# Q and K through the score banks, x2 rebuilt in the expert tiles, plain scatters, and idle products at the head

## The reference

```python
def _lora_proj(x, W, b, A, B):
    return einsum('bsh,oh->bso', x, W) + b + 2.0 * einsum('bsr,or->bso', einsum('bsh,rh->bsr', x, A), B)

q, k, v = proj(layernorm(x)), proj(ctx), proj(ctx)                     # 16 heads of 16
scores = einsum('bqhd,bkhd->bhqk', qh * D ** -0.5, kh) + attn_bias     # attn_bias: 128 x 16 x 128 x 128
attn = einsum('bhqk,bkhd->bqhd', softmax(scores, axis=-1), vh)
x2 = x + tanh(g_xattn[0]) * attn
xf = layernorm(x2)
idx = argmax(softmax(xf @ Wg + bg), axis=-1)                           # one of 8 experts
y = gelu(xf @ W1[idx] + b1[idx], approximate=False) @ W2[idx] + b2[idx]
out = x2 + tanh(g_ffn[0]) * y
```

## Time and profile before

| | us |
|---|---|
| median of 3 runs | 1670.7 (1669.65 to 1671.39) |
| the profiled execution | 1668.51 |
| its span, first to last instruction | 1666.6 |
| first product of scores | 57.73 after the span's start |
| first product of scores of sequence 124 | 1247.33 |
| last product with W1 | 1646.89 |
| PE busy | 1450.7, 87% of the span |
| DVE busy | 1061.8, 64% |
| ACT busy | 887.9, 53% |
| POOL busy | 942.9, 57% |

### The profile page before, as it was taken

How to read it: one execution, slowest core, us unless ns; L and a number is a source line. 1 busy time by engine, 2 the same in 40 slices (tenths; PEclk the granted TensorE clock), 3 DMA queues, 4 the chain that set the end, 5 groups by cost and what they waited for, 6 DMA issues and landing times.

```text
span 1666.6 us, 43159 instructions
## 1 busy us (share of the span) xinstructions
PE 1450.7 (87%) x13374; PEld 1166.7 (70%) x13374; DVE 1061.8 (64%) x2734; ACT 887.9 (53%) x1883; POOL 942.9 (57%) x671
## 2 busy tenths in 40 slices
PE   3789999989989989989998998998997589999886
PEld 2577777777777777777777777777776468777775
DVE  2477787787788788778778778778877311111111
ACT  1466666666666666666666666666664123333231
POOL 2345555555555555556555555555555356666667
PEclk9999999999999999999999999999999699999998
DMA  4355655555555555555555555555552499999994
GB/s 140 85 164 150 178 163 154 171 170 153 166 175 152 163 174 156 160 175 157 157 174 163 157 168 168 155 167 171 154 166 66 139 249 253 242 226 229 230 221 93
DMA packets 383026, 281.53 MB, mean 169 GB/s; under 512 B 21599, under 2 KB 349691, under 8 KB 382972
## 3 DMA queue, kind: packets, MB, share of 16 engines
q1 hardware_dynamic: 356092, 246.22, 50.8%
q0 software_dynamic: 26880, 34.64, 10.5%
HBM read 226.86 MB, written 56.00 MB: 170 GB/s over the span
## 4 chain that ended last, share of the span: by engine, by line
PE 51%; ACT 18%; DMA 15%; issue 10%; DVE 2%; SPq 1%; POOL 1%; ACTq 1%; POOLq 0%; DVEq 0%
DMA out<-og,ids 14%; PE bank L464 9%; PE bank L553 7%; PE bank L569 7%; PE bank L559 7%; ACT KT L642 5%; PE bank L515 5%; PE bank L451 4%; ACT OT L674 4%; ACT x2n L651 3%; ACT xn L651 3%; PE bank L519 3%; ACT PT L658 2%; PE bank L536 2%; PE bank L598 2%
## 5 line engine op out<-in xcount | busy, mean ns | idle before, releaser
L380 POOL TENSOR_TENSOR sc<-sc,negmax 128x1024 f32<-128x1024 f32 x256 | 484.4, 1892 | 435.6 <-DVE negmax L784 435.6
L778 DVE TENSOR_TENSOR sc<-bank,sc 128x512 f32<-128x512 f32 x512 | 337.6, 684 | 195.2 <-PE bank L451 192.4
L658 ACT ACTIVATE PT<-bank 128x512 f32<-128x512 f32 x512 | 293.3, 603 | 59.7 <-PE bank L464 59.7
L784 DVE TENSOR_REDUCE negmax<-sc 128x8 f32<-128x1024 f32 x256 | 312.3, 1220 | 17.0
L420 POOL DMA_INDIRECT out<-og,ids x144 | 223.5, 1552 | 132.3 <-issue 112.0
L464 PE MATMUL bank<-cst,sc 128*128 128x128 f32 x2048 | 273.6, 277 | 0.7 <-ACT PT L658 0.7
L464 PEld LDWEIGHTS bank<-cst,sc 128*128 128x128 f32 x2048 | 226.6, 142 | 43.1 <-issue 41.8
L943 DVE TENSOR_SCALAR og<-bank,tg 128x512 f32<-128x512 f32 x72 | 54.0, 750 | 276.1 <-DMA out<-og,ids 240.5
L687 ACT COPY XT<-bank 128x512 f32<-128x512 f32 x128 | 75.0, 586 | 183.8 <-PE bank L539 183.8
L396 POOL TENSOR_TENSOR rs<-ve,cst 128x2 f32<-128x2 f32 (+1 forms) x135 | 94.8, 703 | 119.4 <-DVE ve L893 98.9
L642 ACT ACTIVATE KT<-bank,bk_half,cst 128x256 f32<-128x256 f32 x256 | 123.7, 564 | 56.5 <-PE bank L569 56.5
(11 more groups left out here) (120 smaller groups left out, 2196.7 us busy)
## 6 DMA issues: line engine op xcount, KB each, us to landing
sc<-in_bias SPq DMA_DIRECT2D x256, 512.0 KB, 5.1
xg<-rows_dram SPq DMA_DIRECT2D x72, 272.0 KB, 4.0
w_sb<-in_w SPq DMA_DIRECT2D x72, 257.0 KB, 4.1
sc<-in_w SPq DMA_DIRECT2D x72, 256.0 KB
ctx_sb<-in_ctx_in SPq DMA_DIRECT2D x128, 128.0 KB, 5.3
x_sb<-in_x SPq DMA_DIRECT2D x128, 128.0 KB, 2.1
out<-x SPq DMA_DIRECT2D x128, 128.0 KB, 1.7
rows_dram<-vacant SPq DMA_DIRECT2D x9, 272.0 KB, 3.6
```

The costliest lines, as they stand in the source:

```text
L380: nc.gpsimd.tensor_tensor(s, s, m, ALU.add).then_inc(sub_ok, 1)
L658: nc.scalar.activation(PT[:, t.slot(2), 512 * q:512 * q + 512], b_t[q % 2][:], ACT.Exp).then_inc(pt_ready, 1)
L778: nc.vector.tensor_tensor(s, b_s[q][:], s, ALU.add).then_inc(s_used, 1)
L784: nc.vector.tensor_reduce(negmax[:, t.slot(2), 8 * h:8 * h + 8], sc[:, t.slot(4), 1024 * h:1024 * h + 1024].rearrange("p (h k) -> p h k", ...
```

## The change

- The products of Q and K go into the first two banks of the scores (`b_s[0]`, `b_s[1]`) once DVE has added the bias to them, and stand between the two halves of the turns; Q is made two steps and K one step ahead of the scores, V three steps ahead. V and the turned x2 use the other two banks. In a step of PE the product with V now comes right after the scores, the attention output and gate after all turns, and V, the turn of x2 and the turns of xn and ctx at the end.
- ACT's order follows: both norms and the copy of `OT` first, V, x2 and XT copies last.
- DVE makes `shift` ahead of `add_bias` 0 and copies `rs` and `shift` of x2 into two spare columns of its row (`x2ln`), for which it waits on the scatter of eight sequences ago.
- SP no longer writes x2 to `out`. An expert tile rebuilds it: DVE takes (xn2 - shift) / rs from the gathered row (`x2g`, two operations of 128 x 256 and a reciprocal a tile) and adds it to the expert's result (one operation in place of L943). The scatters into `out` write and no longer add.
- At the head DVE clears `xgT` and sets V to one in 32 pieces; POOL's memset of V is gone; PE makes 24 idle products of zeros before the low-rank products.

```diff
-        x2 = sb("x2", [P, 8, HID])
+        x2 = sb("x2", [P, 2, HID])
-        b_v, b_x2 = b_s[0], b_s[1]
+        b_v, b_x2 = b_s[2], b_s[3]
...
-                done = seq(i, k, 2)
-                if done:
-                    sp.wait_ge(x2_ok, done.n(1, 1))
-                    sp.nop(nofuse=True)
-                    sp.dma_start(out[done.n()], x2[:, done.slot(8), :]).then_inc(x2_kept[done.slot(8)], 16)
...
-            nc.gpsimd.memset(V[:], 1.0).then_inc(s_setg, 1)
...
-                            og[:, t.slot(2), a, :], None, bounds_check=TOKENS - 1, oob_is_err=False,
-                            compute_op=ALU.add
+                            og[:, t.slot(2), a, :], None, bounds_check=TOKENS - 1, oob_is_err=False
                         ).then_inc(og_out[t.slot(2)], 16)
...
+            pe.wait_ge(s_warm, 1)
+            for n in range(WARM):
+                mm(bank[7][:, 0:P], xgT[:, 0, 0, 0:P], xgT[:, 0, 0, 0:P], start=True, stop=True)
...
+            def project(w, t, first, ready):
+                pe.wait_ge(xt_evac, t.n(1, 2))
+                for o in range(KC):
+                    for c in range(KC):
+                        ins = mm(b_s[o][:, 0:2 * P], W[w][:, c, o * P:o * P + P],
+                                 XT[:, t.k // 2 % 2, first + c, :], start=(c == 0), stop=(c == KC - 1))
+                    ins.then_inc(ready, 1)
...
+                if cur and (qry or ky):
+                    pe.wait_ge(s_used, cur.n(4, 2))
...
+            nc.vector.memset(xgT[:], 0.0).then_inc(s_warm, 1)
+            for n in range(8):
+                for h in range(0, HEADS, 4):
+                    nc.vector.memset(V[:, n, h:h + 4, :], 1.0).then_inc(s_ones, 1)
...
-                if cur:
-                    add_bias(cur, 0)
                 norms = norms_at(i, k - 1)
                 if norms:
                     a, b = norms
                     dve.wait_ge(rs_ok, here.n(1, 5))
...
+                    was_done = seq(i, k, 3)
+                    if was_done:
+                        if was_done.reached(8):
+                            dve.wait_ge(x2_out[was_done.slot(8)], was_done.per(8, 16))
+                        dve.wait_ge(shift_ok, here.n(1, 5))
+                        nc.vector.tensor_copy(x2ln[:, was_done.slot(8), :], ln[:, 1, :]).then_inc(ln_ok, 1)
                 if cur:
+                    add_bias(cur, 0)
                     add_bias(cur, 1)
...
+                    nc.vector.reciprocal(inv[:, t.slot(8), :], xg[:, t.slot(8), :, HID + 1]).then_inc(inv_ok, 1)
+                t = tile(i, k, 1)
+                if t:
+                    dve.wait_ge(inv_ok, t.n(1, 1))
+                    if t.reached(2):
+                        dve.wait_ge(og_ok, t.n(1, -1))
+                    for a in range(HALVES):
+                        nc.vector.tensor_scalar(x2g[:, t.slot(2), a, :], xg[:, t.slot(8), a, 0:HID],
+                                                xg[:, t.slot(8), a, HID + 2:HID + 3], inv[:, t.slot(8), a:a + 1],
+                                                ALU.subtract, ALU.mult).then_inc(x2g_ok, 1)
```

More of the change, by code:

```diff
@@ L218, in flamingo_block @@
         x2_out = [sem(f"x2_out{i}") for i in range(8)]
-        x2_kept = [sem(f"x2_kept{i}") for i in range(8)]
         x2t_ready, x2t_evac = sem("x2t_ready"), sem("x2t_evac")
@@ L235, in flamingo_block @@
         SETUP_DMAS = 21
+        WARM = 24
         SETUP_OPS = 15
@@ L465, in turn @@
                 ins.then_inc(tr_ready, 1)
+            def project(w, t, first, ready):
[5 more added lines that the diff above has]
+                    ins.then_inc(ready, 1)
             def step(i, k):
[L468 to L469 removed]
+                nxt, val, qry, ky, cur, prev, fin, old, gate, grp = (
+                    seq(i, k, lag) for lag in (-4, -3, -2, -1, 0, 1, 2, 3, 4, 5))
+                was_gate = seq(i, k, 5)
                 if cur:
[L471 removed]
+                    pe.wait_ge(v_evac, val.n() if val else N)
                     if gate:
@@ L526, in step @@
                     ins.then_inc(o_ready, 1)
+                if val:
+                    pair, tok = val.k // 2 % 2, P * val.slot(2)
+                    pe.wait_ge(xt_evac, val.n(1, 1))
+                    if cur:
+                        pe.wait_ge(s_used, cur.n(4, 3))
+                    elif val.reached(1):
+                        pe.wait_ge(v_evac, val.n())
+                    mm(b_v[:, 0:HID], top3[:], bv_rows[:], start=True, stop=False)
+                    for c in range(KC):
+                        ins = mm(b_v[:, 0:HID], XT[:, pair, KC + c, tok:tok + P], W["v"][:, c, :],
+                                 start=False, stop=(c == KC - 1))
+                    ins.then_inc(v_ready, 1)
+                if old:
+                    pe.wait_ge(xn2_ok, old.n(1, 1))
+                    if cur:
+                        pe.wait_ge(s_used, cur.n(4, 4))
+                    else:
+                        pe.wait_ge(s_used, 4 * N)
+                        pe.wait_ge(x2t_evac, old.n())
+                    for c in range(KC):
+                        ins = nc.tensor.transpose(b_x2[:, c * P:c * P + P],
+                                                  xn2[:, old.slot(8), c * P:c * P + P], ident)
+                    ins.then_inc(x2t_ready, 1)
                 if nxt:
-                    pair, tok = nxt.k // 2 % 2, P * nxt.slot(2)
                     pe.wait_ge(xn_ok, nxt.n(1, 1))
@@ L648, in normalise @@
                 act.wait_ge(shift_ok, at)
+                if n == 1 and t.reached(8):
+                    act.wait_ge(x2_out[t.slot(8)], t.per(8, 16))
                 if t.reached(2):
```

163 lines of the change are left out of this document (63 added, 100 removed).

## The result

| | before | after |
|---|---|---|
| median of four runs | 1670.2 us | 1583.8 us |
| span of the profiled execution | 1666.6 | 1581.5 |
| first scores | 57.73 | 43.86 |
| from there to the scores of sequence 124 | 1189.6 | 1146.4 |
| from there to the first product with W1 | 71.2 | 77.6 |

The ratio is 0.949 (95% interval 0.947 to 0.952). The forecast was 1602, the range 1560 to 1640: the time is within it, 18 us under the forecast.

What follows compares the result with a forecast made beforehand. PE was taken to bound the attention loop, the `og` scatter ring the expert tiles. Loop -37, head -9, loop's end +3, tiles -22, tail -4 make -69: 1668.5 to 1599.5, median 2.2 above, 1602 us; range 1560 to 1640.

Steps and rivals of the forecast that it cites:

- The ring: Attention loop: work handed round between PE, DVE and POOL needs 9.3 us a step; -37 us over 124 steps.
- R2: Rival, 13%: PE bounds the attention loop, a step takes 8.75 to 8.9 us; 1546 us in all.
- The tiles: Expert tiles: with plain scatters PE bounds at 4.15 us a tile; -22 us (-24 to +17).
- The tail: Behind the last W1 product: 19.7 us become about 15.7; -4 us (0 to -6).
- the first tiles: First eleven expert tiles: paced by SP and by the clearing of tails; 0 us.
- R1: Rival, 18%: POOL or, second, the scatters' landing bounds the expert tiles at 4.4 us a tile; 1617 us.
- the rule on ports: Expert tiles: DVE's two `x2g` operations would hold up POOL's scatters through shared ports; 4.3 us a tile.
- The head: Before the first scores: one Q and one V product less, 7 us, faster low-rank products, about 2.5; sum -9 us.
- The loop's end: Last four attention steps: DVE's own pace now has the power and the copy in it; +3 us (0 to 6).
- The idle products: Head: if PE is then at 2.4 GHz, the low-rank products halve; about 2.5 us off (0 to 3).
- R5: Rival within the forecast's 50%: idle products end too early, the clock falls back, or they delay low-rank products; +3 us.
- R4: Rival, 5% with the like: DVE's wait for an old scatter holds up the attention loop; 1680 us and more.

Runs made afterwards that it cites:

- Experiment 3: Changed kernel with DVE's first bias addition again ahead of `shift` and of the copy of two columns; 1544.8 us, ratio 0.927.
- Experiment 2: Kernel before with scatters into `out` that write instead of add, leaving out the adding of x2 to the experts' result; 1634.5 us, ratio 0.980.
- experiment 8: Changed kernel with the x2 rows of each expert tile rebuilt twice on DVE; 1584.5 us, ratio 0.950.
- experiment 4: On top of experiment 3, the choice of experts moved on DVE behind the second bias addition; 1533.7 us, ratio 0.920.
- experiment 7: On top of experiment 4, PE turns x2 ahead of the product with V, and ACT copies in that order; 1529.2 us, ratio 0.917.
- experiment 1: Changed kernel without PE's 24 idle products, all else kept; 1686.6 us, ratio 1.012.
- experiment 5: Changed kernel with 96 no-operations in place of the idle products, which the build dropped; 1679.4 us, ratio 1.008.
- experiment 6: Changed kernel with the 24 idle products moved from PE's head to just behind the attention loop; 1685.2 us, ratio 1.010.
- 9: Changed kernel with 192 waits for an event long come in place of the idle products; 1585.2 us, ratio 0.950.
- 10: Changed kernel with 34 waits for an event long come in place of the idle products; 1585.9 us, ratio 0.951.

## Why the prediction was right, and where it was not

**The ring (right).** Predicted 9.3 us a step and -37; measured 9.34 and -43. The two kinds of step fit too: 8.9 and, with the expert choice, 10.5 were forecast; 8.75 to 9.19 and 10.34 to 10.64 came. PE waits where it was said to, at L468 for the bias addition, 71.0 us / 124 = 0.57 a step; in the eight steps from 705.63, 2.9 of 4.8 us stand in the two steps with the choice. The chain goes through the ring's members in the order of the sum: bias additions 1.3, projection 1.96, second turns 0.87, attention output and gate 0.82, DVE's own part 2.4, the power with its hand-overs 0.90, `shift` and the copy 0.39. One working in it does not come out: 2.6 less 1.25 is 1.35 and not 1.15, and as the choice hides only the power's 0.9, its own numbers give 2.6 - 0.9 = 1.7. The steps with the choice are 1.4 to 1.7 longer, with the position products in it. Experiment 3 takes the power on POOL out of the ring's way, and 39 us go. Of the 6 us beyond the forecast, 3.7 lie at the start: the first sixteen steps fall from 147.1 to 138.6 us, 0.53 each, the later ones from 9.65 to 9.33, 0.32 each.

**R2, PE bounds the loop (false here, true one edit on).** It was given 13% at 8.75 a step. With the bias addition in its old place PE does bound the ordinary step, at 8.34 to 8.73, under the 8.75 that I had worked out. I had got PE's need by taking two waits off the step, which leaves every smaller gap in it; adding up its rows would have been closer.

**The tiles (right).** Predicted 4.15 apart and -22; measured 4.11 and -24.5. The share of the software queue fell to 16.2%, forecast 17. The landing no longer stands in DVE's waits, 10.8 us in three waits. Experiment 2 gives the gain without any other part of the change: -24 in the 60 tiles and -6.5 behind them.

**The tail and the first tiles.** -6.5 for -4, -3.4 for 0. The stretch to the twelfth tile took 53.6 to 56.6 us in the versions with the same tile code, so only 0.7 of the 3.4 us lie outside the spread of one and the same code. POOL's four last scatters cost 0.98 + 0.30 each, not 1.86; I had the shorter issue in rows 10 and used the longer one for the tail and for R1. With it, POOL needs 2.6 us of a tile's 4.11, and R1's first half could not have bound. Rows 10 were read wrongly besides: the issue at 1303.39, which I called alone, also had a DVE operation beside it (timeline of DVE):

```profile
1303.90 1.35 DVE L917 TENSOR_TENSOR past<-row,end 1x1152 f32<-1x1152 f32 x1
```

and still took 0.96. What made the one at 1304.65 longer they don't show.

**R1 and the rule on ports.** Rows first: experiment 8's issue beside `x2g` took 1.12 for 0.98 us, and started in the middle of the first of the two operations, which take 0.40 us each. The Trainium skill (SBUF — State Buffer, Who interferes with whom) has `tensor_scalar` in a two-port mode and GpSimd exclude each other for the whole instruction. No run shows which mode these operations ran in, so the 0.14 us neither confirm nor contradict that rule; they show that these two operations do not hold the issue up in this kernel. That the rule holds for GpSimd's computing operations no run here shows either.

**The head (right sign, a term missed).** -13.9 for -9 (its terms, 7 and 2.5, add up to 9.5). I had counted a Q and a V at 7; the last V and Q before the scores took 1.90 and 2.12 us from start to start, so 4.0, and another 3.2 us are PE's pace, which was full some us sooner in this execution (K 1.89 us for 3.34). Most of the rest I had missed. It is in the kernel before, in PE's timeline, at its turns of xn:

```profile
35.16 0.69 PE L536 MATMUL bank<-cst,xn 128*128 128x128 f32 x2 [0.96 <-ACT xn L651]
...
43.93 0.41 PE L536 MATMUL bank<-cst,xn 128*128 128x128 f32 x2 [1.46 <-ACT QT L631]
...
52.35 0.41 PE L536 MATMUL bank<-cst,xn 128*128 128x128 f32 x2 [2.56 <-ACT KT L642]
```

0.96 + 1.46 + 2.56 = 5.0 us of waits. Each of these turns needs two things of ACT: the copy that empties `b_x`, and the norm of the next sequence, which stood behind that copy. The third one, in ACT's timeline:

```profile
49.84 1.93 ACT L642 ACTIVATE KT<-bank,bk_half,cst 128x256 f32<-128x256 f32 x4 [2.76 <-PE bank L569]
51.65 0.60 ACT L651 ACTIVATE xn<-x_sb,shift,rs 128x256 f32<-128x256 f32 x1
```

The copy ends at 51.77, the norm at 52.25, PE starts at 52.35. So most of the wait is the shared bank and 0.5 us the norm. The change gives Q and K other banks and puts the norms first; I had read both for the loop alone.

**The loop's end (too low).** +6.4 for +3. 4.4 us of it lie between the scores of sequences 124 and 127, whose three steps take 10.07, 7.48 and 7.22 in place of 7.99, 5.95 and 6.47: there is nothing left to put beside the power, and it is paid in full, as the sum said, with more than I took. The other 2.0 us lie behind them. With no bias addition left to fill DVE's queue, `shift` stands behind a pick and a power, ACT's exponentials behind the norms that need it, and PE waits 4.69 us at 1229.43, after which its granted clock is 0.50: the turns there take 1.94 us in place of 1.09. The clock falls at the loop's end of the kernel before as well (turns of 1.95 at 1284.04).

**The idle products (the term about right, what they are worth missed).** I gave them -2.5 us (0 to 3) through the clock, and R5, that they end too early and the clock falls back, +3. The profiles of five versions have them, and PE's head is the same in all. In the changed kernel's own profile R5 came true; in that of experiment 4 the forecast did (timeline of PE):

```profile
1.97 8.56 PE L427 MATMUL bank<-xgT 128*128 128x128 f32 x48 [1.97 <-DVE xgT L720]
11.50 1.12 PE L431 MATMUL bank<-bq,aq 8*128 8x256 f32 x4 [0.98 <-DMA cnt<-in_bg]
```

| profile | PE idle before the low-rank products | these, four pieces each | first scores |
|---|---|---|---|
| changed kernel | 2.51 | 1.84, 1.91, 1.91 | 43.86 |
| experiment 7 | 2.21 | 1.23, 1.91, 1.91 | 43.91 |
| experiment 3 | 1.70 | 1.13, 1.02, 1.75 | 42.25 |
| experiment 8 | 1.40 | 1.13, 1.02, 1.14 | 42.26 |
| experiment 4 | 0.98 | 1.12, 1.02, 1.02 | 39.57 |
| no early products (1, 5, 6, 9, 10) | | 2.04 to 2.07, 1.91, 1.91 | 42.38 to 45.34 |

So early products do speed up the low-rank ones, by up to 2.6 us, the more the shorter the gap between them was; and how long they themselves take (7.04 to 8.56 us), and with it the gap, varies from profile to profile. The first scores come at 39.57 to 43.91 with them. In time it can't be told: 1583.8 us against 1585.2 and 1585.9 with waits in their place. What the recorded theory of experiment 1 says, that they did not gain, was read from one profile.

What I gave nothing, without a reason, is the place of the code. As 96 instructions ahead of the loop the idle products are worth 103 us (experiments 1, 6, 9, 10): the rest of the change shortens the code ahead of the loop by 34 instructions and puts it in a bad place. Nothing in the rows of before could show that, since its instruction queue had 29 packets too; but a change of code ahead of a long loop was a rival that I did not name. Without them it would have ended at 1687, outside the range. That the forecast held rests on this luck as much as on its sum.

The Trainium skill (TensorE: Matmul & The Clock Gate, What's actually happening) has the clock rise with activity. The table above agrees, as far as the pace goes. The profile of the changed kernel agrees with the fall: the granted clock is 0.50 from 12 us on, after the idle 2.5 us and through PE's 13 idle us behind the low-rank products, and 1.00 again from about 39 us, in the midst of its first dense work.

**The sum.** The span fell by 85 us where I had 69. Against the forecast the ring gave 6 us more, the head 5, the tiles 2.5, the tail 2.5, the first tiles 3.4 more, the loop's end 3.4 less. The last 2 us are the median, which stands 0.4 above its profiled execution where I had added 2.2. The lower end of the range was called half of R2's gain beyond the forecast; half would be 1574, and 1560 is three quarters. With 1574 the time would still be inside.

**R4.** DVE's wait for the old scatter never shows in the waits. **Open:** why the bad place is bad. The runs show that it recurs with one block of 16 KB, that, by the loop's end, it reaches at most 0.24 of a block ahead of the boundary (18.76 is good) and less than 0.06 behind it, and that nine blocks are fetched a round although the loop covers seven. What the fetching rule is, they don't show.

## What to carry to other kernels

Look at the instruction queue on the page before and after every edit: packets beyond one pass over the program mean that a loop is fetched anew. An edit ahead of a long loop, even of dead work, can bring that about or cure it, and move the time by far more than what it does. One pass on the page before, as here, does not rule it out. And read an effect of a few us from several profiles, not from one. When two engines hand work to each other several times a step, add up the ring, not the engines; the cheapest cure is to put an operation that needs nobody under another engine's turn, as the bias addition under POOL's power (-39 us). If a helper's stores must add to what is there, compare with reading the addend on chip: the adding scatter took 2.9 times the queue share per MB.

## What the runs showed of the hardware

- PE's loop of 1601 instructions (100 KB) ran with one pass of fetches in some places and lost 7.8 to 8.4 us a round in others, at an equal count of instructions in all (experiment 6 against the changed kernel, 7562 both). Where it lies relative to blocks of 16 KB decides.
- An adding scatter: 40.6% of the DMA engines for 5.65 MB, a plain one 16.2% for 6.44; its issue on POOL 1.56 us, plain 0.98.
- Waits for an event long past, two to an instruction, held PE for about 0.11 us an instruction: 392 of them put the low-rank products at 23.19 us, 512 at 29.92, in place of 11.6. 192 put them at 12.43; the head's loads hid the rest.
- The row of the clock and PE's pace disagree in the first 40 us. In the kernel before PE ran Q at half pace (3.62 us for 1.89) at 38.85 while the rows show a granted clock of 1.00; in experiment 5, under the same 1.00, it ran Q at full pace (1.99).
